# The last stage of an attention and token-selection kernel, cut into quarters of four image pairs

## What is computed

```
x = x + _L0_conv_ref(_gn(x), ...)    # shifted 8x8 window attention with a feed-forward layer
x = x + _L1_conv_ref(_gn(x), ...)    # the layer that the last stage ends
```

```
scores = jnp.einsum('gbcl,gc->gbl', xb, conv_w)
p = e / jnp.sum(e, axis=-1, keepdims=True)          # e = exp(scores)
_, idx = jax.lax.top_k(p, K)                        # 6 pixels of each block
gath = jnp.take_along_axis(out, idx_s[:, :, None, :], axis=-1)
feat = jnp.concatenate([gath..., st], axis=-1)      # 6*64 gathered values and 64 mask values
h = jax.nn.relu(feat @ W1 + b1)                     # 448 -> 448
rec = (h @ W2 + b2).reshape(NB, n, OC, LH, LW)      # 448 -> 7 channels x 64 pixels of the block
...
return jnp.einsum('bohw,co->bchw', grid, out_w)     # 7 -> 64 channels, added to x
```

## Time and profile before

| | |
|---|---|
| median of three runs | 780.2 us (779.53 to 784.32) |
| span of the profiled execution | 778.6 us, first to last instruction |
| its own time beside the span | not listed; the median is 1.6 us above the span |
| gathers begin / all of `feat` is there | 695.98 / 709.8 us |
| first and second layer end on PE | 723.8 / 736.9 us |
| first mix starts / last addition ends | 741.1 / 762.5 us |
| first store issued / end of the span | 746.35 / 778.6 us |
| mean granted TensorE clock | 0.923 of full |

### The profile page before, as it was taken

How to read it: one execution, slowest core, us unless ns; L and a number is a source line. 1 busy time by engine, 2 the same in 40 slices (tenths; PEclk the granted TensorE clock), 3 DMA queues, 4 the chain that set the end, 5 groups by cost and what they waited for, 6 DMA issues and landing times. The chain is left out here.

```text
span 778.6 us, 21192 instructions
## 1 busy us (share of the span) xinstructions
PE 665.7 (86%) x8584; PEld 371.4 (48%) x8584; DVE 516.4 (66%) x997; ACT 480.4 (62%) x963; POOL 355.1 (46%) x441
## 2 busy tenths in 40 slices
PE   4785789999999999999998579999999988749880
PEld 2562455565565555655555232233333367735350
DVE  4796487877777787877778322577777786372181
ACT  3565266777777777777775548877777656624000
POOL 4696446778777777788776520022221123100000
PEclk9787599999999999999999959999999999969955
DMA  9550000000000000000000020122112220120278
GB/s 216 137 128 11 1 3 2 3 2 3 2 3 3 3 3 3 3 2 3 3 2 3 2 56 1 28 55 56 33 50 55 55 55 2 31 72 2 63 194 269
DMA packets 15719, 31.44 MB, mean 40 GB/s; under 512 B 7488, under 2 KB 9284, under 8 KB 15620
## 3 DMA queue, kind: packets, MB, share of 16 engines
q1 hardware_dynamic: 12592, 29.16, 14.1%
q10 hardware_dynamic: 2760, 0.66, 0.5%
q0 software_dynamic: 272, 0.27, 0.2%
HBM read 20.71 MB, written 9.37 MB: 39 GB/s over the span
## 5 line engine op out<-in xcount | busy, mean ns | idle before, releaser
L794 POOL TENSOR_TENSOR sc<-sc,mx 128x512 f32<-128x512 f32 x128 | 133.7, 1044 | 102.4 <-DVE mx L725 102.4
L722 DVE TENSOR_TENSOR sc<-s_ps,bias_tab 128x512 f32<-128x512 f32 x128 | 87.7, 685 | 52.6 <-PE s_ps L528 52.6
L1424 POOL TENSOR_TENSOR square<-xs 128x1024 f32<-128x1024 f32 x16 | 34.1, 2133 | 165.5 <-DVE xs L1166 165.5
L539 PE MATMUL t_ps<-consts,sc 128*128 128x128 f32 x512 | 84.4, 288 | 16.2 <-ACT pt L656 12.5
L656 ACT ACTIVATE pt<-t_ps 128x512 f32<-128x512 f32 x128 | 75.7, 592 | 31.2 <-PE t_ps L539 30.1
L539 PEld LDWEIGHTS t_ps<-consts,sc 128*128 128x128 f32 x512 | 54.3, 142 | 84.8 <-issue 48.1
L725 DVE TENSOR_REDUCE mx<-sc 128x8 f32<-128x512 f32 x128 | 87.8, 686 | 4.4
L1081 ACT ACTIVATE hs<-h_ps,fb1s 128x512 f32<-128x512 f32 x128 | 78.2, 689 | 19.1 <-PE h_ps L990 19.0
L528 PE MATMUL s_ps<-kx,qu 32*64 32x128 f32 x2048 | 72.3, 278 | 3.5 <-DVE kx L749 2.9
L990 PE MATMUL h_ps<-xs,fw 64*128 64x512 f32 x256 | 68.7, 650 | 1.0 <-ACT hs L1081 1.0
L528 PEld LDWEIGHTS s_ps<-kx,qu 32*64 32x64 f32 x2048 | 56.7, 134 | 15.2 <-issue 13.4
(11 more groups left out here) (207 smaller groups left out, 1295.2 us busy)
## 6 DMA issues: line engine op xcount, KB each, us to landing
raw<-in_x_dram SPq DMA_DIRECT2D x32, 256.0 KB, 5.1
xr<-in_x_dram SPq DMA_DIRECT2D x32, 256.0 KB, 3.9
out_dram<-x SPq DMA_DIRECT2D x32, 256.0 KB, 3.9
rec_scratch<-r SPq DMA_DIRECT2D x4, 224.0 KB, 2.5
w<-in_L_conv_W_dram SPq DMA_DIRECT2D x1, 784.0 KB
w<-in_L_conv_W_dram SPq DMA_DIRECT2D x1, 672.0 KB
xs<-rec_scratch SPq DMA_DIRECT2D x16, 28.0 KB
xs<-rec_scratch ACTq DMA_DIRECT2D x16, 28.0 KB
```

What stands on the lines that cost most here:

```text
L539: last = pe.transpose(t_ps[:, m], sc[n % KEPT][:, m].rearrange("c h k -> c (h k)"), ident)
L722: dve.tensor_tensor(sc[n % KEPT][:, :, :, :], s_ps[j][:, :, :, :], bias_tab[:, j, hp], ALU.add)\
L794: pool.tensor_tensor(v, v, mx[n % KEPT][:, :].unsqueeze(2).broadcast_to([128, 8, TOK]), ALU.subtract)\
```

## The change

The stage from the gathers on works in four quarters k of four pairs (128 rows each). Right behind the first four gathers' transposes PE does the first layer of quarter 0, and the second layer behind one more gather; the other gathers follow. The matmuls of the first layer have 128 columns in place of 512, four times as many. Of `rec` each quarter has its own transfers: two out (`rec_away`, 64 partitions each) and four back (`rec_back`, 14 partitions each), those of quarter 0 on SP, of the others on ACT among its relus. The mixes of quarters 0 and 1 stand between the layers of later quarters; `mix_bank` gives half 1 of quarters 2 and 3 the banks 0 to 3, all other mixes the banks 4 to 7. A store is half a picture of two pairs (256 KB as before, in pieces of 2 KB a channel). `rec` has memory of its own. The diff, cut to its core:

```diff
-            rec_out = [sem(stage, f"rec_out{h}") for h in range(2)]
-            rec_in = [sem(stage, f"rec_in{h}") for h in range(2)]
+            rec_out = [sem(stage, f"rec_out{k}") for k in range(QUARTERS)]
+            rec_in = [sem(stage, f"rec_in{k}") for k in range(QUARTERS)]
...
+            hid = sb(stage, "mlp_hid", [MT, 2, 4, ROWS])
+            rec = sb(stage, "rec", [128, QUARTERS, OUTDIM])
...
+            def hidden_bank(m):
+
+                return psb[m // 2][0:MT, ROWS * (m % 2):ROWS * (m % 2 + 1)]
+
+            def rec_away(eng, k):
+
+                eng.wait_ge(s["rec"], k + 1)
+                away = rec_dram[ROWS * k:ROWS * (k + 1), :].rearrange("(n a) o -> a n o", a=2)
+                for a, (lo, hi) in enumerate(HALVES):
+                    eng.dma_start(away[a], rec[lo:hi, k]).then_inc(rec_out[k], 16)
+
+            def rec_back(eng, k):
+
+                eng.wait_ge(rec_out[k], 32)
                 for q in range(4):
...
+                    row = ROWS * k + 2 * BLOCKS * q
+                    src = rec_dram[row:row + 2 * BLOCKS].rearrange("(g a) (o l) -> (a o) g l", a=2, l=TOK)
+                    dst = grid[32 * q:32 * q + 2 * OC, k].rearrange("o (g l) -> o g l", l=TOK)
+                    eng.dma_start(dst, src).then_inc(rec_in[k], 16)
+
+            def mix_bank(k, half, q):
+
+                return psb[q if k >= 2 and half == 1 else 4 + q]
...
-                    for p in range(PAIRS):
-                        store(p)
+                    def stores(k):
+                        for half in range(2):
+                            at = slice(COLS * half, COLS * (half + 1))
+                            for q in range(0, 4, 2):
+                                sp.wait_ge(s["added"], 8 * k + 4 * half + q + 2)
+                                duo = slice(4 * k + q, 4 * k + q + 2)
+                                for a, (lo, hi) in enumerate(HALVES):
+                                    sp.dma_start(out_pairs[a, :, duo, at], x1[lo:hi, duo, at]).then_inc(s["stored"], 16)
+                    rec_away(sp, 0)
+                    rec_back(sp, 0)
+                    for k in range(QUARTERS):
+                        stores(k)
...
+                    for k in range(1, QUARTERS):
+                        relu(k)
+                        if k >= 2:
+                            rec_back(act, k - 1)
+                        rec_away(act, k)
+                    rec_back(act, QUARTERS - 1)
...
+                    def first_layer(k, parts=range(4)):
+                        pe.wait_ge(s["feat_a"], 2 * k + 2)
+                        pe.wait_ge(s["feat_b"], 2 * k + 2)
...
+                    first_layer(0)
+                    gather(4)
+                    second_layer(0)
+                    for n in range(5, 8):
+                        turn_back(n - 2)
+                        gather(n)
+                    turn_back(6)
+                    turn_back(7)
+                    mix(0, 0)
+                    first_layer(1)
+                    mix(0, 1)
+                    second_layer(1)
+                    first_layer(2)
+                    second_layer(2)
+                    first_layer(3, range(0, 2))
+                    mix(1, 0)
+                    first_layer(3, range(2, 4))
+                    mix(1, 1)
+                    second_layer(3)
+                    for k in range(2, QUARTERS):
                         for half in range(2):
                             mix(k, half)
```

More of the change, by code:

```diff
@@ L1541, in spread_feat, with quarter @@
                 return last
-            def spread_rec(eng, h, a):
-                eng.wait_ge(rec_out[h], 32)
-                rows = rec_dram[256 * a + 128 * h:256 * a + 128 * (h + 1)]
-                for q in range(4):
[L1548 to L1552, removed]
+            def quarter(k):
+                return slice(C * k, C * (k + 1))
+            def hidden_bank(m):
[7 more added lines that the diff above has]
+                eng.wait_ge(rec_out[k], 32)
+                for q in range(4):
+                    row = ROWS * k + 2 * BLOCKS * q
[4 more added lines that the diff above has]
+                return psb[q if k >= 2 and half == 1 else 4 + q]
             with nc.Block() as block:
@@ L1672, in spread, with take_gathered @@
                         spread_feat(copy, n, 1).then_inc(s["feat_b"], 1)
-                    for n in range(8):
+                    def take_gathered(n):
                         act.wait_ge(s["gathered"], n + 1)
@@ L1727, in turn_back, with second_layer @@
                         last.then_inc(s["feat_ps"], 1)
[L1728 to L1745, removed]
+                    def first_layer(k, parts=range(4)):
+                        pe.wait_ge(s["feat_a"], 2 * k + 2)
+                        pe.wait_ge(s["feat_b"], 2 * k + 2)
+                        for m in parts:
+                            cols, to = slice(MT * m, MT * (m + 1)), hidden_bank(m)
+                            if m % 2 == 0:
+                                after(pe, s["hid"], 4 * (k - 1) + m + 2)
+                            for j in range(TOP // 2):
+                                pe.matmul(to, w1[:, j, cols], feat[:, j, :, quarter(k)], start=(j == 0), stop=False)
+                            last = pe.matmul(to, w1s[:, cols], st_t[:, :, quarter(k)], start=False, stop=True)
+                            if m % 2 == 1:
+                                last.then_inc(s["hid_ps"], 1)
+                    def second_layer(k):
+                        after(pe, s["rec"], k - 1)
                         for m in range(4):
-                            last = pe.matmul(psb[4 + i][:, 0:OUTDIM], hid[:, m, 128 * t:128 * (t + 1)], w2[:, m],
+                            pe.wait_ge(s["hid"], 4 * k + m + 1)
+                            last = pe.matmul(psb[2 + k % 2][:, 0:OUTDIM], hid[:, k % 2, m], w2[:, m],
                                              start=(m == 0), stop=(m == 3))
@@ L1751, in mix @@
                     def mix(k, half):
-                        after(pe, s["added"], 8 * (k - 1) + 4 * (half + 1))
+                        pe.wait_ge(rec_in[k], 64)
+                        if k == 0 and half == 0:
+                            pe.wait_ge(s["gathered_copied"], 8)
+                            pe.wait_ge(s["feat_a"], 8)
+                            pe.wait_ge(s["feat_b"], 8)
+                        elif k == 2 and half == 1:
+                            pe.wait_ge(s["hid"], 16)
+                            pe.wait_ge(s["rec"], QUARTERS)
+                        else:
+                            pe.wait_ge(s["added"], 4 * (2 * k + half - (1 if k < 2 or k == 2 and half == 0 else 2) + 1))
                         for y in range(2):
@@ L1756, in mix @@
                                 blk = grid[rows, k].rearrange("o (y x h w) -> o y h x w", y=4, x=4, h=8)[:, 2 * half + y]
-                                last = pe.matmul(psb[2 * q + half][:, 256 * y:256 * (y + 1)], ow[rows, :], blk,
+                                last = pe.matmul(mix_bank(k, half, q)[:, 256 * y:256 * (y + 1)], ow[rows, :], blk,
                                                  start=True, stop=True)
                         last.then_inc(s["mixed"], 1)
[L1760 to L1763, removed]
+                    gather(0)
+                    gather(1)
+                    turn_back(0)
+                    gather(2)
+                    turn_back(1)
+                    gather(3)
+                    turn_back(2)
+                    pe.wait_ge(s["st_copied"], 1)
+                    pe.wait_ge(tail_in, 16 * len(tail_loads))
+                    first_layer(0)
+                    gather(4)
+                    second_layer(0)
+                    for n in range(5, 8):
+                        turn_back(n - 2)
[13 more added lines that the diff above has]
+                    second_layer(3)
+                    for k in range(2, QUARTERS):
                         for half in range(2):
```

72 lines of the change are left out of this document (43 added, 29 removed).

## The result

The changed kernel takes 777.6 us (median of 20, 772.09 to 781.28) where the kernel before took 781.49 beside it (20 runs, 778.21 to 784.32): **ratio 0.9942 [0.9925, 0.9959]**, about half a per cent faster. The forecast was 766.4, 0.981 of these 781.49, and its range (759 to 772) missed the median. Its first gather starts at 697.72, 1.74 later than in the profile of before; from there to the end it is 75.6 us, where before had 82.6 (778.6 − 695.98). To set a time of after against the forecast, subtract 1.74.

A forecast was written before the change was run, and what follows sets the result against it. Bound: a serial line of gathers, both layers, `rec`'s trip and first mix, then additions and stores. Quarter 3's first store at 754.35 plus 10.5 us gives span 764.85; the median 1.6 above is 766.4 us, range 759 to 772.

The forecast's parts named there:

- 3.6 us back in a quiet stretch, 5.9 in all: Trip of `rec` through DRAM with nothing beside it: 2.3 us out, then four issues and a 2.5 us landing back.
- I take the 4.3, so 5.35 us back: Way back of `rec` for quarters 2 and 3, amid stores: landing taken as 4.3 us, 5.35 with the issues.
- 0.75 us of cover, so no cost: PE at `mix(1,0)`: `rec` 1 back at 733.2, before PE gets there at 733.95, so no wait.
- the first rival: Stores starve the way back of `rec` on shared DMA engines; `rec` 3 back by 754.65, time 770; chance 0.13.
- Half pictures: Stores in 2 KB instead of 4 KB pieces might run badly; at 130 GB/s the time would be 788; chance 0.04.
- the quieter cases: End of the span: 763 with quiet trips only and `mix(3,0)` at full clock, 761 if new stores run at 380 GB/s.
- a 769: Time if weight loads hold up the first layer, 4.7 us a quarter, making PE's chain 2.8 us longer.
- old trips: Each trip of `rec` costs 9.4 us as before, PE stands 4 us and its clock falls; time 776; chance 0.08.
- The lanes: Way back of `rec` on 14 of 16 DMA engines: a quarter's 224 KB take 1.5 us, 3.0 without the rule.

The follow-up runs named there:

- stores held: Changed kernel with SP holding every store until the last quarter's `rec` is back in grid; 787.3 us in one run, span 785.5.
- the changed kernel again: The changed kernel with nothing altered, run for a second profile; 775.3 us (6 runs), ratio 0.991 to the kernel before.
- quarter 2 held: Changed kernel with SP holding only quarter 2's stores until `rec` 3 is back; 779.05 us, ratio 0.9957 to the kernel before.
- the run without trips: Changed kernel without `rec_away` and `rec_back`, mixes waiting only for their quarter's bias addition, output not right; 765.43 us, ratio 0.9778 to the kernel before.
- the waits filled: Changed kernel with 16 identity transposes on PE ahead of `mix(0,0)` and of `mix(1,0)`; 773.55 us, ratio 0.9902 to the kernel before.

## Why the prediction was wrong

**The step that failed is the trip of `rec`**: "3.6 us back in a quiet stretch, 5.9 in all", and for the quarters 2 and 3 "I take the 4.3, so 5.35 us back". Quiet trips are 6.9 to 7.8 us (stores held); in after they are 7.6 for `rec` 0, 9.4 for `rec` 1, 12.0 and 12.1 for `rec` 2 and 3 (`rec` 3 had been priced 3.3 + 5.35 = 8.65). Of `rec` 2's 12.0 some 3 are a wait on ACT behind quarter 3's relus, which the forecast had as well (2.5). Against the forecast the shift along the chain builds up so, in before's coordinates:

| | forecast | after − 1.74 | later by |
|---|---|---|---|
| `mix(0,0)` starts | 716.2 | 717.85 | 1.7 |
| `mix(1,0)` starts | 733.95 | 737.02 | 3.1 |
| `rec` 3 ready | 742.35 | 745.89 | 3.5 |
| `mix(3,0)` starts | 751.0 | 758.03 | 7.0 |
| end | 764.85 | 771.56 | 6.7 |

Of the 6.7 us, 1.7 are `rec` 0's trip, 1.4 `rec` 1's, 0.4 the layers behind it, and 3.5 `rec` 3's; the last stretch gives back 0.3. The other 4.5 between forecast and median are 1.74 of later start in this profile and 2.75 that the median lies further above the span (4.3 us, where 1.6 was taken over from before): the profiled execution is 1.8 us longer than its span, and 2.5 under the median. What causes these 4.5 isn't shown. Clock lost behind PE's waits in other executions (1.7 us at `mix(0,0)` in the changed kernel again, 5.7 behind `mix(1,0)` with quarter 2 held) is of that size; how many of the timed runs lost it isn't recorded.

**In quarter 0** the median landing of the old `rec` transfers (2.5 us) was taken for the last of four. In after the last was issued at 716.44 and landed 3.1 us later, one issue on SP took 1.24 us where 0.36 was priced, and the second transfer out left 0.5 us behind the first: 2.8 out and 4.8 back (priced 2.3 and 3.6). The landing of 3.1 lies inside the bounds that were given, 1.9 to 4.80, and 0.6 above the choice; the issues cost as much again.

**In quarter 1** the forecast had "0.75 us of cover, so no cost", with both ways at their quiet price. Here it was wrong in the place of the stores as well: quarter 0's run at 220 GB/s from 723 to 733, amid the way out of `rec` 1 (4.66 us in place of 2.3). The stores had been followed only to their first issue, not to their end. PE waited 1.82 us at `mix(1,0)` with half a layer, `mix(1,1)` and the second layer of quarter 3 queued behind it.

**In quarter 3** the way out took 4.4 (2.3 and 1 us were priced) and the way back 7.7 (5.35). The ceiling of the first rival (the stores of quarter 2 are through when it lands) did hold in kind: the DMA engines run dry at 760, when `rec` 3 is back. It came later than worked out because quarter 1's stores began some 3 us late behind `mix(1,0)`, and the stores of the two quarters, amid the trips of `rec` 2 and 3, ran from some 743 to 760 where 14.5 us had been priced.

**The order on PE** made these trips dear. The two early mixes were costed at their own 1.1 us each; that an in-order engine gives their wait to everything behind them was seen for `mix(1,0)` only and priced at nothing. Shown by the order alone: with `rec` 3's trip still 10.9 us long, the mixes behind the next layers are at 0.9832 and 0.9826, where 0.981 had been forecast.

**What held.** First layer 3.50 us a quarter (703.50 to 707.00; priced 3.76), second layer 3.22 (3.07), a mix at full clock 1.15 (1.1) and at half 2.13 (2.12), first store 26.0 us before the old one (27.75 forecast). Half pictures cost at most 1.2 us. The sums of the working are sound but for two that change nothing here: the 763 and 761 of the quieter cases are spans, beside a forecast and a 769 that are times (1.6 more), and the old trips' end, 760 plus 2.12, 1.25 and 10.5, is 773.9 and not 774.4. Of the rivals the second (old trips, 776) came nearest to the median, but not by its price: its 9.4 us lie between the short trips and the long ones, and it gives `mix(0,0)` 719.7 where 717.85 was measured. Its clock fall behind a wait of PE did occur, in some executions. That both mechanisms of the first two rivals could act together, each in part, was the case that no rival had.

**The lanes.** By the Trainium skill, "DMA: Bandwidth & Descriptors", section "Why a DMA increments its semaphore by 16 and not by 1", a transfer of 14 partitions would run on 14 engines. With nothing else on the queues the profile with all stores held shows a share of 0.54 and 123 GB/s while four such transfers are in flight:

```profile
749.00:751.00 2.00, 0.00 (x0) 0.00 (x0) 1.57 (x3) 0.00 (x0) 0.00 (x0) 0.54 0.54 123
```

That is more than the 74 GB/s of the old 7-partition ones and far from the 380 of 128 partitions; it agrees by half, and no run here tells lanes from short pieces.

**What stays open.** Why the issue of one small transfer sometimes takes 1.2 us (715.16 on SP, 752.40 on ACT); in the second case stores were in flight, in the first only the same way back's first piece. And why the clock falls behind a short wait in one execution and not in another.

## What to carry to other kernels

Price a round trip through DRAM under the transfers that will run beside it, followed to their end, and by the last of its pieces, not by their median. In an in-order queue, put work that waits for such a trip behind work that doesn't: here moving four mixes on PE (and two bias additions on DVE) was worth 0.8 to 1.1%, as much as the change itself had brought (0.6 to 0.9%). A wait on PE that looks like 2 us may be dearer, since the clock can fall behind it (1.7 us more in one profile here, nothing in another).

## What the runs showed of the hardware

- The granted clock fell to 0.5 while PE was working, 1.5 to 2 us behind an idle stretch of 2.1 and of 2.5 us (the changed kernel again), and in the run without trips behind two waits of 0.7 and 1.0 us (714.7 to 717.0; 0.50 at 719 to 721). In the first profile of after it stayed at 1.0 behind a wait of 2.36 us. With the waits filled it was 1.0 up to 750, in one profile; that the filler kept it there isn't shown, since the first profile of after had the same without it.
- Reading the moving columns of a float32 matmul of 128 columns in strides ("c n a") took 0.137 us a record (0.82/6), in order 0.109 (0.66/6).
- With nothing beside them, two transfers of 64 partitions took 2.8 us from the bias to their landing, one of 128 partitions and the same bytes 2.0.
